# One PSUM bank moved from the ring of scores and projections to the ring that ScalarE empties

## The chip, the cores and the metric

The kernel runs on one core of one Trainium2 chip. The metric is the device time of one execution in microseconds (us), lower is better. The engines are TensorE (PE in the rows, with its weight loads as PEld), VectorE (DVE), ScalarE (ACT), GpSimd (POOL) and the DMA queues, which SyncE (SP) issues here.

## The reference, cut to what matters

Sixteen sequences of 256 rows with 128 channels go through a small wavelet and linear-attention stage (the prologue), and then through four layers of attention and mixture of experts:

```
for l in range(4):
    h = rms(x, ln1[l]); q, k, v = h @ wq[l], h @ wk[l], h @ wv[l]      # 16 query heads, 4 key heads of 64
    q, k = rope(q), rope(k)
    p = softmax(q k^T / 8 + causal_bias)                                # 256 x 256 for each head
    x = clip(x + (p v) @ wo[l], -100, 100)
    h = rms(x, ln2[l]); 2 of 8 experts for each row, by softmax(h @ wr[l])
    x = clip(x + sum(share_e * (silu(h wg_e) * (h wu_e)) @ wd_e), -100, 100)
out = x1 + gb * x
```

## The kernel before, in words

Every engine has its own program, written out by hand, and semaphores tie them together. The main part is a loop over 64 steps, one for each layer and sequence (`it`), and in each step TensorE's program mixes work of three steps: the scores of `it`, the last half of the attention of `it - 1`, and the projections of `it + 1`. The attention of a step falls into four blocks `q` of four heads.

TensorE's row of work in a step is: scores(it, 0), place 0, attend(it-1, 2), place 1, scores(it, 1), attend(it-1, 3), the projection of v, place 2, the output projection, place 3, turn_h, scores(it, 2), project_qk(it+1) outputs 0 to 5 (with the transposes of the routed rows after output 3), place 4, attend(it, 0), the router's logits, place 5, scores(it, 3), place 6, project_qk outputs 6 to 9, attend(it, 1), the ranks, place 7. The eight places hold pieces of the experts' work of the eight steps before: an even piece transposes rows and gated values, an odd one computes gate, up and down products. Of each eight steps (numbered 0 to 7 by `it % 8`, from `it` = 9 on), step 1 has pieces in places 4 to 7, steps 2 to 4 in all places, steps 5 and 6 in all but place 6, steps 7 and 0 in none. Pieces are odd in the odd places in steps 1 to 5, and the other way round in step 6 in places 0 to 5.

A block of attention goes like this:

- `scores` (L719 on, products at L734): for the heads i = 0, 2 of the block it computes the short product of head i (128 keys), that of head i + 1, then the long products (256 keys) of both, which tell VectorE that the bank is full. Each head has a PSUM bank.
- `mask_and_max` on VectorE (L1547, L1549): reads each head's bank twice, adds the mask and takes the maximum, and frees the bank; `L1553` then gives the negated maxima.
- `exps` on ScalarE (L1030), `invert` on VectorE (L1558), `normalise` on GpSimd (L1264).
- `attend` on TensorE: for each of the four heads three transposes into one bank (L759), which `copy_probs` on ScalarE copies out (L1037); then `weigh` for heads 0 and 1 when the copy of head 1 is done, and for heads 2 and 3 when the copy of head 3 is done (L777, L779).

`project_qk` (L807 to L809) gives each of its ten outputs a bank, which `rope` on VectorE (L1527) reads and frees; on VectorE rope of outputs 0 to 5 comes after the mask and maximum of block 2, and rope of outputs 6 to 9 after those of block 3, after invert(it, 2) and after what VectorE does of place 6.

The eight banks are three rings. The s ring holds scores, q/k projections and the output projection. The t ring holds the transposed probabilities, v, the transposed h and routed rows, logits, ranks and the experts' y, all of which ScalarE empties. The u ring holds the weighed values and the experts' rows, gate and gated values. `number_slots` counts the uses of each ring in TensorE's order; use n takes bank n modulo the ring's size, and TensorE waits until use n minus the ring's size has been read. The wait for a head's scores bank is:

```
def bank_is_free(i):
    at_least(pe, "s_free", S_AT["head", it, q, i] - S_RING + 1)
```

Of the kernel before, what the change touches and what calls it, by code (L numbers as in the profile page):

```python
# [207 lines left out]
def bass_program(nc, I, out):  # L208
    ctx = ExitStack()
    with ctx:  # L210
# [207 lines left out]

        half_steps = half_step_places()
        S_AT, T_AT, U_AT = number_slots(half_steps)  # L420
        S_RING, T_RING, U_RING = 4, 2, 2

        def s_bank(key):
            return S_AT[key] % S_RING
# [1348 lines left out]
```

How the kernel before makes its waits and increments, by code:

```python
        def phase_done(eng, k):  # L405
            eng.wait_ge(sem("phase_end"), PH * (k + 1))
# [1 line left out]
        def at_least(eng, name, n):  # L409
            if n > 0:
                eng.wait_ge(sem(name), n)
# [19 lines left out]
        def s_is_full(eng, key):  # L432
            eng.wait_ge(sem("s_full"), S_AT[key] + 1)
# [1 line left out]
        def t_is_full(eng, key):  # L435
            eng.wait_ge(sem("t_full"), T_AT[key] + 1)
# [1 line left out]
        def u_is_full(eng, key):  # L438
            eng.wait_ge(sem("u_full"), U_AT[key] + 1)
# [1 line left out]
        def s_was_read(eng, key):  # L441
            eng.wait_ge(sem("s_free"), S_AT[key] + 1)
# [1 line left out]
        def t_was_read(eng, key):  # L444
            eng.wait_ge(sem("t_free"), T_AT[key] + 1)
# [1 line left out]
        def u_was_read(eng, key):  # L447
            eng.wait_ge(sem("u_free"), U_AT[key] + 1)
# [28 lines left out]
        @block.sync  # L477
# [19 lines left out]
            def load_wv(l):  # L497
                load(wv, I["wv"][l], "wv_in")
            def load_wo(l):
                load(wo, I["wo_blocks"][l].rearrange("(c p) n -> p c n", p=P), "wo_in")
            load_wv(0)
            load_wo(0)
            load(wr, I["L0_ffn_wr"].rearrange("l h n -> h l n"), "wr_in")
            sp.wait_ge(sem("zeros_ready"), 1)
            for rows in rows_in + rows_out:
                for q in range(ZERO_PIECES):
                    sp.dma_start(zero_piece(rows, q), zeros).then_inc(sem("rows_zeroed"), 16)
            for h in range(2):
                sp.wait_ge(sem("x1_ready"), h + 1)
                sp.dma_start(x1_kept[:, half(h), :], x1[:, half(h), :]).then_inc(sem("x1_stored"), 16)
            def load_piece(it):
```

## Time and profile before

| | us |
|---|---|
| median of 3 runs | 3653.08 (3648.91 to 3657.68) |
| the profiled execution | 3653.33 |
| its span | 3651.5 |
| prologue, up to the scores of step 0 | 244.25 |
| steps 0 to 8 (no experts' pieces) | about 372 |
| last eight steps' experts and output, after the loop | 236.5 |
| TensorE busy | 2906.2 |
| mean granted TensorE clock | 0.906 |

The profile is of one execution. An instruction's row has its start from the span's beginning, its duration, its engine and line; in brackets stands the idle time of the engine just before it, and what ended it. Matmuls are pipelined, and their ends are modelled, so that two rows can overlap. The granted clock is 1.00 at 2.4 GHz and 0.50 at 1.2 GHz.

### The profile page before, as it was taken

The page shows a single profiled execution, that of the slowest core. Times are in us where ns is not written, and L with a number is a line of the kernel's source. Part 1 is how long each engine was busy: PE and PEld are TensorE (multiplying, and loading weights), DVE is VectorE, ACT ScalarE, POOL GpSimd, SP SyncE. Part 2 cuts the span into 40 slices and gives each one's busy share as a digit, 9 for nine tenths or more (in the row PEclk, how much of TensorE's full clock was granted, in tenths as well). Part 3 has the DMA queues.
Part 4 walks back from the last instruction along what each step waited for, and adds up shares of the span by engine and source line. Part 5 has one row for each costly group of instructions (what it writes and reads, how often), then busy time and mean ns, then how long its engine had stood idle before and what let it go on. Part 6 is the DMA issues. An engine that isn't in the chain of part 4 may idle for free.

```text
span 3651.5 us, 69801 instructions
## 1 busy us (share of the span) xinstructions
PE 2906.2 (80%) x22326; PEld 2366.8 (65%) x22326; DVE 2193.6 (60%) x8164; ACT 2016.6 (55%) x7089; POOL 1858.4 (51%) x1671
## 2 busy tenths in 40 slices
PE   5238887888888887888888987888888988888673
PEld 2226666777667766777667766777667766777462
DVE  5775555665556655665556665666566665666343
ACT  3026666566655665665656565656566665656321
POOL 0035655444655466554655556554655565555413
PEclk9569999999999999999999999999999999999775
DMA  9110101443145421543245421453145411442374
GB/s 375 74 41 31 35 33 59 146 150 122 52 133 175 153 84 61 169 148 117 67 136 169 155 78 61 164 165 97 67 137 179 163 56 62 153 154 80 115 251 137
DMA packets 270444, 438.36 MB, mean 120 GB/s; under 512 B 36305, under 2 KB 155633, under 8 KB 268657
## 3 DMA queue, kind: packets, MB, share of 16 engines
q1 hardware_dynamic: 253696, 400.31, 33.1%
q0 software_dynamic: 16384, 33.59, 3.0%
q8 instruction: 182, 2.98, 0.3%
q14 instruction: 182, 1.48, 0.1%
HBM read 323.13 MB, written 110.62 MB: 119 GB/s over the span
## 4 chain that ended last, share of the span: by engine, by line
PE 58%; ACT 19%; DVE 10%; POOL 6%; issue 3%; DMA 2%; SPq 1%; POOLq 0%; DVEq 0%
ACT arena L1030 10%; PE psum L759 7%; PE psum L777 7%; PE psum L807 5%; PE psum L808 4%; PE psum L809 4%; PE psum L734 4%; PE psum L779 3%; PE psum L827 3%; ACT arena L1037 3%; PE psum L877 3%; PE psum L878 2%; PE psum L879 2%; PE psum L903 2%; PE psum L902 2%
## 5 line engine op out<-in xcount | busy, mean ns | idle before, releaser
L1264 POOL TENSOR_TENSOR arena<-arena 128x512 f32<-128x512 f32 (+1 forms) x512 | 744.0, 1475 | 729.6 <-DVE arena L1558 727.7
L1030 ACT ACTIVATE arena<-arena 128x128 f32<-128x128 f32 (+1 forms) x2048 | 901.0, 446 | 23.6 <-DVE arena L1553 23.6
L759 PE MATMUL psum<-arena 128*128 128x128 f32 x3072 | 475.5, 292 | 259.0 <-ACT arena L1037 230.7
L759 PEld LDWEIGHTS psum<-arena 128*128 128x128 f32 x3072 | 342.9, 145 | 373.0 <-ACT arena L1037 293.4
L1037 ACT COPY arena<-psum 128x384 f32<-128x384 f32 x1024 | 445.5, 480 | 237.7 <-PE psum L759 236.7
L1562 DVE COPY arena<-psum 128x512 f32<-128x512 f32 x256 | 177.1, 692 | 618.4 <-PE psum L779 616.3
L734 PE MATMUL psum<-arena 64*128 64x128 f32 (+1 forms) x4096 | 453.5, 365 | 0.1
L1549 DVE CUSTOM_DVE_ANT_0 arena<-psum,arena 128x256 f32<-128x256 f32 x1024 | 430.2, 420 | 0.0
L807 PE MATMUL psum<-h_hi,wqk_hi 128*128 128x256 f32 x1280 | 392.8, 307 | 45.2 <-DVE arena L1549 43.7
L1527 DVE TENSOR_TENSOR arena<-psum,arena 128x512 f32<-128x512 f32 x640 | 406.0, 681 | 26.2 <-PE psum L809 21.3
L1280 POOL TENSOR_TENSOR arena<-arena 128x512 f32<-128x512 f32 x320 | 400.6, 1278 | 8.7 <-DVE arena L1527 8.6
L1030 ACT ACTIVATION_READ_ACCUMULATOR arena<-arena 128x1 f32 x2048 | 390.3, 191 | 0.0
L808 PE MATMUL psum<-h_hi,wqk_lo 128*128 128x256 f32 x1280 | 372.8, 291 | 0.0
L809 PE MATMUL psum<-h_lo,wqk_hi 128*128 128x256 f32 x1280 | 371.4, 290 | 0.0
L777 PE MATMUL psum<-arena 128*64 128x256 f32 x2048 | 368.2, 442 | 0.0
L734 PEld LDWEIGHTS psum<-arena 64*128 64x128 f32 x4096 | 321.3, 205 | 50.8 <-issue 25.6
L1255 POOL DMA_INDIRECT rows_in<-arena x256 | 256.2, 1001 | 150.3 <-DVE arena L1606 91.7
L807 PEld LDWEIGHTS psum<-h_hi,wqk_hi 128*128 128x128 f32 x1280 | 255.7, 200 | 93.1 <-issue 87.0
L1547 DVE CUSTOM_DVE_ANT_0 arena<-psum,arena 128x128 f32<-128x128 f32 x1024 | 294.0, 287 | 22.9 <-PE psum L734 15.7
L808 PEld LDWEIGHTS psum<-h_hi,wqk_lo 128*128 128x128 f32 x1280 | 256.6, 200 | 0.0
L809 PEld LDWEIGHTS psum<-h_lo,wqk_hi 128*128 128x128 f32 x1280 | 253.9, 198 | 0.0
L1112 ACT ACTIVATE arena<-psum 128x512 f32<-128x512 f32 x160 | 95.4, 596 | 270.5 <-PE psum L879 268.0
(199 smaller groups left out, 5711.0 us busy)
## 6 DMA issues: line engine op xcount, KB each, us to landing
gu<-gu_kept SPq DMA_DIRECT2D x320, 512.0 KB, 4.3
wd<-wd_kept SPq DMA_DIRECT2D x320, 256.0 KB, 3.9
arena<-rows_in SPq DMA_DIRECT2D x320, 64.0 KB
rows_out<-arena SPq DMA_DIRECT2D x320, 64.0 KB
rows_in<-arena SPq DMA_DIRECT2D x34, 512.0 KB, 7.8
rows_out<-arena SPq DMA_DIRECT2D x34, 512.0 KB, 7.1
gu_kept<-w_hi SPq DMA_DIRECT2D x32, 256.0 KB
gu_kept<-w_lo SPq DMA_DIRECT2D x32, 256.0 KB
```

The costliest lines, as they stand in the source:

```text
L734: return T.matmul(psum[:, s_bank(("head", it, q, i)), cols], QKT[par][r, 2 + 2 * q + i // 2, rows * P:(rows + 1) * P], QKT[par][r, q // 2, ...
L759: mm = T.transpose(psum[:, t_bank(key), j * P:(j + 1) * P], probs[:, q, i, j * P:(j + 1) * P], ident)
L777: return T.matmul(psum[r, bank, c0:c0 + S], v[:, 0, kv], pt[:, 0:S], start=True, stop=False, skip_group_check=True)
L807: T.matmul(out, wqk_hi[:, cols], h_hi, start=True, stop=False)
L808: T.matmul(out, wqk_lo[:, cols], h_hi, start=False, stop=False)
L809: mm = T.matmul(out, wqk_hi[:, cols], h_lo, start=False, stop=True)
L1030: ins = A.activation(a, a, ACT.Exp, bias=negmax[:, q, k:k + 1], accum_out=rowsum[:, q, k:k + 1])
L1037: A.copy(probsT[:, 4 * (q % 2) + i, :], psum[:, t_bank(key), 0:3 * P]).then_inc(sem("t_free"), 1)
L1264: ins = G.tensor_tensor(a, a, r[:, :, t:t + 1].broadcast_to([P, 4, P * (t + 1)]), ALU.mult)
L1280: G.tensor_tensor(QKT[it % 2][:, 2 * u:2 * u + 2, :].rearrange("p a b -> p (a b)"), own_part[:, k, :], turned_part[:, k, :], ALU.add).then ...
L1527: V.tensor_tensor(dst.rearrange("p (i s) -> p i s", i=2), psum[:, s_bank(("qk", it, m)), :].rearrange("p (i s) -> p i s", i=2), table.rear ...
L1549: V.tensor_tensor_reduce(probs[:, q, i, P:3 * P], psum[:, s_bank(key), P:3 * P], mask, SCALE, -3.0e38, ALU.add, ALU.max, rowmax[:, q, 2 * ...
```

## The change: ring sizes

```
-        S_RING, T_RING, U_RING = 4, 2, 2
+        S_RING, T_RING, U_RING = 3, 3, 2
```

That is the whole diff. Every engine's instructions stay the same and in the same order. What differs are bank numbers and the values that TensorE's waits for a free bank compare with: a use of the s ring now waits for the reading of the use three before it, not four, and a use of the t ring for the reading of the use three before it, not two. The u ring keeps banks 6 and 7. The prologue names its banks itself.

## Rows read from the trace of the kernel before

**Rows 1.** The page, busy time of an engine and share of the span.

```profile
PE 2906.2 (80%) x22326; PEld 2366.8 (65%) x22326; DVE 2193.6 (60%) x8164; ACT 2016.6 (55%) x7089; POOL 1858.4 (51%) x1671
```

**Rows 2.** The page, the chain that ended last, by engine.

```profile
PE 58%; ACT 19%; DVE 10%; POOL 6%; issue 3%; DMA 2%; SPq 1%; POOLq 0%; DVEq 0%
```

**Rows 3.** Waits of TensorE: us in total, times, longest.

```profile
PE psum L759 <- ACT arena L1037: 230.7, 240, 2.8
PE psum L792 <- ACT arena L1063: 221.0, 64, 68.1
PE psum L807 <- DVE arena L1549: 43.7, 60, 1.9
```

**Rows 4.** Stretches: steps 8 to 62, then step 50, step 51.

```profile
core 0: us, PE busy (x) PEld busy (x) DVE busy (x) ACT busy (x) POOL busy (x), PEclk, DMA share, GB/s
573.91:3371.60 2797.69, 2400.71 (x19040) 1968.12 (x19037) 1728.13 (x6857) 1694.71 (x6044) 1549.41 (x1387) 0.94 0.37 121
...
2696.83:2749.33 52.50, 46.05 (x383) 38.60 (x382) 34.92 (x130) 33.49 (x116) 29.24 (x27) 1.00 0.54 174
2749.33:2804.85 55.52, 49.07 (x382) 40.61 (x381) 34.86 (x130) 33.59 (x116) 29.31 (x27) 0.94 0.51 164
```

**Rows 5.** Timeline of TensorE, attend(36, 1): start, us, idle before.

```profile
2039.86 0.82 PE L759 MATMUL psum<-arena 128*128 128x128 f32 x6
2040.91 0.93 PE L759 MATMUL psum<-arena 128*128 128x128 f32 x6 [0.24 <-ACT arena L1037]
...
2042.48 0.60 PE L777 MATMUL psum<-arena 128*64 128x256 f32 x4
```

**Rows 6.** Timeline of ScalarE in the same block.

```profile
2040.38 0.86 ACT L1037 COPY arena<-psum 128x384 f32<-128x384 f32 x2 [0.71 <-PE psum L759]
2041.50 0.86 ACT L1037 COPY arena<-psum 128x384 f32<-128x384 f32 x2 [0.26 <-PE psum L759]
```

**Rows 7.** Timeline, scores(39, 0), and VectorE waiting for them.

```profile
2153.38 1.58 PE L734 MATMUL psum<-arena 64*128 64x128 f32 x16
...
2154.34 0.29 DVE L1547 CUSTOM_DVE_ANT_0 arena<-psum,arena 128x128 f32<-128x128 f32 x1 [0.54 <-PE psum L734]
```

**Rows 8.** Timeline, scores(36, 2) and what follows on both engines.

```profile
2020.57 1.58 PE L734 MATMUL psum<-arena 64*128 64x128 f32 x16
2022.67 0.36 PE L807 MATMUL psum<-h_hi,wqk_hi 128*128 128x256 f32 x1 [0.52 <-DVE arena L1549]
...
2021.89 0.28 DVE L1547 CUSTOM_DVE_ANT_0 arena<-psum,arena 128x128 f32<-128x128 f32 x1
...
2024.42 3.71 DVE L1527 TENSOR_TENSOR arena<-psum,arena 128x512 f32<-128x512 f32 x6
```

**Rows 9.** Timeline, scores(36, 3), last output projected (L807), mask, rope.

```profile
2034.74 1.58 PE L734 MATMUL psum<-arena 64*128 64x128 f32 x16
2039.13 0.28 PE L807 MATMUL psum<-h_hi,wqk_hi 128*128 128x256 f32 x1
...
2035.70 0.29 DVE L1547 CUSTOM_DVE_ANT_0 arena<-psum,arena 128x128 f32<-128x128 f32 x1
...
2040.21 2.47 DVE L1527 TENSOR_TENSOR arena<-psum,arena 128x512 f32<-128x512 f32 x4
```

**Rows 10.** Timeline of TensorE, the third head's transposes in attend(35, 3), attend(36, 2).

```profile
2008.80 0.92 PE L759 MATMUL psum<-arena 128*128 128x128 f32 x6 [2.02 <-ACT arena L1037]
...
2051.52 0.92 PE L759 MATMUL psum<-arena 128*128 128x128 f32 x6 [2.20 <-ACT arena L1037]
```

**Rows 11.** Timeline of TensorE, output 6 in step 38, without place 6.

```profile
2145.48 0.36 PE L807 MATMUL psum<-h_hi,wqk_hi 128*128 128x256 f32 x1 [0.97 <-DVE arena L1549]
```

**Rows 12.** Timeline, scores(38, 0) and their mask; GpSimd's normalise(40, 3) in step 41.

```profile
2100.78 1.58 PE L734 MATMUL psum<-arena 64*128 64x128 f32 x16
...
2102.75 0.28 DVE L1547 CUSTOM_DVE_ANT_0 arena<-psum,arena 128x128 f32<-128x128 f32 x1
...
2245.75 2.90 POOL L1264 TENSOR_TENSOR arena<-arena 128x512 f32<-128x512 f32 x2 [0.38 <-DVE arena L1558]
```

## The prediction

> **What bounds the kernel now.** I read the busy times first, then the chain that ended last, TensorE's waits, and the timeline of steps 36 to 41 piece by piece. TensorE is busy 80% of the span [rows 1] and holds 58% of the chain, ScalarE 19%, VectorE 10% [rows 2]: a step is a relay in which TensorE mostly works, and now and then waits for ScalarE. Two of its waits are long in total: third and later transposes of a block for ScalarE's copies (231 us, 240 times), and turn_h for scaled rows (221 us, one of 68 us in the prologue); that for a scores bank is 44 us [rows 3]. A step with pieces in all places takes 52.50 us at a granted clock of 1.00, and 55.52 us at 0.94 [rows 4], the same work.
>
> **The t ring, 2 to 3.** In a block the first two heads' transposes start at 2039.86, the third's only at 2040.91, after the first copy [rows 5]. ScalarE copies two heads in 0.86, then idles until 2041.50, and copies the other two by 2042.36 [rows 6]; the last weighing starts at 2042.48 [rows 5]. With a third bank the third head is transposed at once, the four copies run on end: two rows of 0.86 less an overlap, a copy every 0.38, so that the last starts 1.14 after the first and not 1.50 (2041.50 + 0.38 - 2040.38). Its transposes, started when the first copy ends (0.48 + 0.06 after its start), have it full 0.52 later (2039.86 to 2040.38 is that latency), at 1.06, just in time. The gain is 0.37 a block. The same holds where ScalarE comes late, since its pause is inside the block. There are 256 blocks: 94.7. In steps without pieces the next block waits for GpSimd's scatter and normalise, which take no notice: I take off 15 blocks for steps 0 and the first eight, and 2 us for the step whose turn_h then waits for gathered rows. Left: -87 us. Bounds: 0 (if the last transposes miss their time) and -130 (0.5 a block).
>
> **The s ring, 4 to 3, inside a block.** Head 3's short product now waits until VectorE has read head 0 of the same block. Head 0's reading starts 0.96 after the block where VectorE is free (2153.38 to 2154.34) [rows 7], and a bank is back at TensorE 0.78 after its reading started (2021.89 to 2022.67) [rows 8]. Of the block's 1536 columns 640 are then left, 0.63 of about 1.5 us. So the block ends 0.96 + 0.78 + 0.63 = 2.37 after its start, not 1.5: 0.85 later. VectorE's third head, which it takes 1.1 after the first, comes 0.5 later. What follows depends on the block.
>
> Blocks 0 and 1: TensorE then idles 2.20 or 2.02 for ScalarE's first copy [rows 10], so 0.85 is hidden, and ScalarE is behind with earlier exponentials, so the later maxima are too. The cover is gone where VectorE comes late. In step 6 of eight it starts head 0 at 2102.75, 1.97 after the scores [rows 12], and the piece behind is an odd one, that ScalarE waits for: head 3 waits until 2103.53, 1.8 lost, and about 0.3 is given back since there the block behind also waited for the bank of y: +1.5, seven times. In step 1 VectorE first lays out the experts' tiles, and GpSimd's normalise waits for its reciprocal [rows 12] and sends for the rows that the rest of the step waits for: that is 0.5 late, and hides its two attention gains (0.75): +1.2, seven times. Together +19.
>
> Block 2: the projection starts at 2022.67 already waiting for head 0 [rows 8]; now head 3 does, and the projection starts at 23.30, +0.63. Outputs 1 and 3 then wait for readings that are 0.5 late (rope starts at 2024.9 in place of 2024.42 [rows 8], and output 3 needs output 0 read): +0.2. Nothing waits longer behind it until attend(it, 0), for which ScalarE waits. +0.85, all 64 steps: +54. Bounds 0.5 and 1.1.
>
> Block 3: with place 6 filled and even (steps 2 to 4, 21 in all) head 3 starts at 2035.70 + 0.78 = 2036.48 and the scores end 0.85 late. The last output, at 2039.13 before, could start at 2039.98, but needs output 6 read, and rope starts at 2040.21, 0.62 each [rows 9]: 2040.21 + 0.62 + 0.15 = 2040.98. Rope waits for ScalarE's exponentials and piece, which this doesn't move. +1.85: +39. In step 1 the same with VectorE 1.2 later: +1.75, seven times, +12. In the other 36 steps output 6 already waits for head 0 [rows 11]; it starts 0.66 later, and output 9 waits for rope of output 6, itself 0.5 late: +0.9: +32. Block 3 together +84, all on the path, since attend(it, 1) has ScalarE waiting 0.71 [rows 6]. Bounds 50 and 110.
>
> Sum without the clock: -87 + 19 + 54 + 84 = +70.
>
> **The clock.** Steps 50 and 51 differ by 3.0 us through clocks of 1.00 and 0.94, and the 2797.69 us of the main part have 0.94 in the mean [rows 4]: by that ratio low stretches cost about 151 us there now. They follow TensorE's long idles, among them the 2.0 to 2.2 us before the third head's transposes [rows 10]. The change breaks those in two, 0.85 in the scores and about 1.0 before the fourth head: fewer low stretches behind blocks 0 and 1. It lengthens the idle around block 2 (a wait before turn_h stays, and 1.2 in the scores joins it) and makes new ones in block 3. I take -25 and +15. The estimate is rough, from no row of the new idles; bounds -90 and +60.
>
> Sum +60 on the profiled execution's 3653.33, which stands at the median of the runs (3653.08): 3713 us.
>
> **The rivals.**
> A, the other side: the clock. If the low stretches behind waits nearly all go, and block 2 and 3 make none, the clock gives more than 70 back, and the kernel is faster. It decides from 47 fewer stretches of 1.5 us each (half of 3.0). For it: the 2.0 to 2.2 idles do stand before many slow weighings. Against: turn_h's waits, 221 us in total [rows 3], stay, and what is slow behind them stays slow. If 100 of the 151 went: 3653 + 70 - 100 = 3623.
> B: more clock loss. The new pauses of 0.85 in each scores block, close to other waits, pull the clock down in blocks 2 and 3, where TensorE sets the pace: one stretch of 1.5 in half of 64 steps, +48, and none lost: 3653 + 70 + 48 = 3771. For it: step 36's slow weighings come after mere 2 us of idle.
> The Trainium skill, "TensorE: Matmul & The Clock Gate", section "A second HAM failure mode: psum-queue depth-cycling", says that short pauses of the PE between groups of matmuls, from cycling through PSUM banks, make its clock swing between the two levels and cost throughput. By that rule B is the likelier, and the sum would be about +118; the rows show swings now (0.94) behind idles of 2 us, and no row shows one behind a pause of 0.85 alone.
> C: the scores' waits are hidden. If VectorE's readings come so early that blocks 2 and 3 lose only the projection's 0.5 in block 2 (+32): 3653 - 87 + 32 = 3598. Against it: VectorE starts head 0 at the earliest 0.96 after the block begins, while head 3 is wanted at about 0.9.
> D: the rings are no limit and nothing moves: 3653. Against it: both waits stand in the rows.
>
> **How the numbers follow.** My forecast has 0.72 (its own range 3678 to 3745), B 0.13, A 0.08, C 0.03, D 0.04. A difference under 0.2%, 7 us, can't be told from none. Faster takes A and C less what of A ends near zero, 0.10; same 0.04; slower 0.86. The range leaves out C, most of A and the far part of B: 3668 to 3758.
>
> **What would show it.** In the profile after: inside a block the copies (L1037) run on end, four at 0.38, and TensorE's wait for them falls from 231 us to near 120; L734 shows idle on VectorE's L1549 in nearly all 256 blocks, about 0.8 each, some 200 to 250 us; L807 waits on L1527 or L1549 once in block 3, about 1 us in steps 2 to 4; step 50 takes about 53.8 at a clock of 1.00. Wrong would be: L734 not waiting, the fourth output of block 3 not waiting for rope, or a main-part clock above 0.97 (A) or under 0.92 (B).

## The result, and the profile after

The change makes the kernel slower: 3734.15 us (3733.45 to 3734.92, 4 runs) against 3655.3 (3648.91 to 3657.68, 4 runs beside it), a ratio of 1.0219 [1.0201, 1.0236]. The forecast was 3713 with a range of 3668 to 3758, so the result lies inside it, 21 us above the likeliest value. The profiled execution after takes 3733.57 us, 80.24 more than that of before, with a span of 3731.8 and a mean granted clock of 0.904 (0.906 before).

The busy times and the chain of the page of after, which answer to [rows 1, 2]:

```profile
PE 3011.5 (81%) x22326; PEld 2469.1 (66%) x22326; DVE 2201.8 (59%) x8164; ACT 1991.7 (53%) x7089; POOL 1860.7 (50%) x1671
...
PE 56%; ACT 18%; DVE 12%; POOL 7%; issue 4%; DMA 2%; SPq 1%; POOLq 0%; DVEq 0%
```

The counts are the same. TensorE's busy time is 105 us longer for the same work, because the modelled rows are longer: a block's scores, one row of 1.58 before [rows 9], are two rows of 1.14 and 0.92 with a pause between them, and at the low clock the first of the two takes 1.76 (both shown below). In the chain VectorE has gone from 10 to 12%.

TensorE's waits after (us in total, times, longest), which answer to [rows 3]:

```profile
PE psum L792 <- ACT arena L1063: 213.4, 64, 68.1
PE psum L734 <- DVE arena L1549: 207.4, 257, 4.4
PE psum L759 <- ACT arena L1037: 54.1, 70, 1.9
...
PE psum L807 <- DVE arena L1527: 14.3, 21, 0.7
```

The wait for ScalarE's copies has fallen from 231 us to 54. In its place stands one that did not exist: the scores (L734) wait for VectorE's reading of the same block, 257 times, 207 us. The projection no longer waits for the scores' banks (44 us before), only 21 times for rope, which are the steps 2 to 4 with place 6 filled.

Step 50 after, to be set beside its 52.50 in [rows 4]:

```profile
2767.14:2820.88 53.74, 47.93 (x383) 39.83 (x382) 34.97 (x130) 33.07 (x116) 29.54 (x27) 1.00 0.53 170
```

Now a block as it runs. TensorE, scores(35, 1) with attend(34, 3) behind it, after (start, us, idle before):

```profile
2001.14 1.14 PE L734 MATMUL psum<-arena 64*128 64x128 f32 x10
2002.80 0.92 PE L734 MATMUL psum<-arena 64*128 64x128 f32 x6 [0.52 <-DVE arena L1549]
2003.65 1.20 PE L759 MATMUL psum<-arena 128*128 128x128 f32 x9
2005.55 0.55 PE L759 MATMUL psum<-arena 128*128 128x128 f32 x3 [0.70 <-ACT arena L1037]
```

The idle of 2.0 us before the third head's transposes [rows 10] is in pieces: 0.52 inside the scores, 0.70 before the fourth head. Three heads are now transposed on end (x9). Block 3 of the same step, the last two outputs of the projection and attend(35, 1):

```profile
2033.22 0.92 PE L734 MATMUL psum<-arena 64*128 64x128 f32 x6 [0.52 <-DVE arena L1549]
...
2037.76 0.39 PE L807 MATMUL psum<-h_hi,wqk_hi 128*128 128x256 f32 x1 [0.68 <-DVE arena L1527]
...
2038.58 1.61 PE L759 MATMUL psum<-arena 128*128 128x128 f32 x12
```

and ScalarE's copies of that block, which answer to [rows 6]:

```profile
2039.10 1.63 ACT L1037 COPY arena<-psum 128x384 f32<-128x384 f32 x4 [2.61 <-PE psum L759]
```

Four copies take 1.63 on end; before it was 0.86, a pause of 0.26, and 0.86. That is the gain. The projection's wait for rope, 0.68, and the scores' 0.52 are the price in this block.

**Where the time went, step by step.** I cut a step at four points: first product of scores(it, 0), first product of scores(it, 1), turn_h (L792), first product of scores(it, 3). The four pieces hold blocks 0, 1, 2 and 3 in this order. First two steps before, 44 at full clock and 51 with low stretches (columns as in [rows 4]):

```profile
2399.99:2410.59 10.60, 8.39 (x70) 6.48 (x69) 5.91 (x24) 6.92 (x24) 8.89 (x9) 1.00 0.87 281
2410.59:2426.38 15.79, 12.73 (x105) 10.85 (x104) 8.88 (x32) 12.61 (x49) 5.19 (x6) 1.00 0.42 134
2426.38:2440.95 14.57, 13.64 (x112) 11.78 (x112) 10.27 (x40) 6.42 (x18) 8.77 (x8) 1.00 0.37 122
2440.95:2452.46 11.51, 11.27 (x98) 9.47 (x97) 9.61 (x36) 7.32 (x26) 5.94 (x5) 1.00 0.49 160
2749.33:2761.34 12.01, 9.80 (x69) 7.61 (x68) 5.81 (x24) 6.92 (x24) 9.99 (x10) 0.86 0.86 277
2761.34:2778.74 17.40, 14.33 (x106) 11.74 (x105) 8.89 (x32) 12.71 (x49) 4.06 (x5) 0.90 0.39 125
2778.74:2793.33 14.59, 13.66 (x112) 11.80 (x112) 10.54 (x40) 6.63 (x18) 9.33 (x8) 1.00 0.38 122
```

Then two steps after, 35 at full clock, and 51:

```profile
1990.90:2001.14 10.24, 8.84 (x69) 6.78 (x69) 6.17 (x24) 6.81 (x24) 8.25 (x9) 1.00 0.92 286
2001.14:2016.56 15.42, 13.16 (x105) 11.14 (x104) 8.98 (x32) 12.50 (x49) 5.43 (x6) 1.00 0.51 165
2016.56:2031.57 15.01, 14.06 (x113) 12.09 (x113) 10.69 (x40) 6.54 (x18) 9.34 (x8) 1.00 0.34 118
2031.57:2044.63 13.06, 11.86 (x99) 9.81 (x98) 9.30 (x36) 7.22 (x26) 6.30 (x5) 1.00 0.43 142
2820.88:2831.12 10.24, 8.84 (x70) 6.79 (x69) 5.90 (x24) 6.82 (x24) 8.28 (x9) 1.00 0.83 258
2831.12:2846.55 15.43, 13.17 (x105) 11.15 (x105) 8.98 (x32) 12.51 (x49) 5.44 (x6) 1.00 0.59 184
2846.55:2863.88 17.33, 16.94 (x113) 14.44 (x113) 10.84 (x40) 6.53 (x18) 9.35 (x8) 0.80 0.32 103
```

Read the clock column. In step 51 before, the low clock stands in pieces one and two (0.86, 0.90) and not in three. After, one and two run at 1.00, and piece three at 0.80, which costs 17.33 - 15.01 = 2.3 us. Compare the full-clock pieces of 44 and 35 to have the change alone: -0.36, -0.37, +0.44, +1.55, together +1.26.

Summed over the 63 steps whose four pieces are complete, after less before is -23.9, -50.2, +107.3 and +53.4 us, together +86.6; prologue and tail give -6.4. The time that the pieces spend at the low clock (worked out as in the next section) sums to 106, 103, 152 and 7 us before, and to 41, 12, 339 and 14 after. So block 2 had low stretches before the change too, and now has more than twice as much; blocks 0 and 1 lost three quarters of theirs. The sum over the loop has hardly moved (369 and 406 us), and the main part's mean clock is 0.94 in both.

### The profile page after: what moved, and what is told of

Read it like the earlier page. It is cut to its first block, busy times and chain, and to the rows that moved or that the text cites. A ratio compares the mean times of both kernels' runs of the same rounds, so it can differ in the third digit from the quotient of the medians.

```text
span 3731.8 us, 69800 instructions
## 1 busy us (share of the span) xinstructions
PE 3011.5 (81%) x22326; PEld 2469.1 (66%) x22326; DVE 2201.8 (59%) x8164; ACT 1991.7 (53%) x7089; POOL 1860.7 (50%) x1671
## 4 chain that ended last, share of the span: by engine, by line
PE 56%; ACT 18%; DVE 12%; POOL 7%; issue 4%; DMA 2%; SPq 1%; POOLq 0%; DVEq 0%
ACT arena L1030 10%; PE psum L759 7%; PE psum L777 6%; PE psum L734 5%; PE psum L807 5%; PE psum L808 4%; PE psum L809 4%; PE psum L827 3%; PE psum L779 3%; PE psum L877 3%; POOL rows_in L1255 2%; PE psum L879 2%; PE psum L878 2%; PE psum L903 2%; PE psum L902 2%
## 5 line engine op out<-in xcount | busy, mean ns | idle before, releaser
L734 PE MATMUL psum<-arena 64*128 64x128 f32 (+1 forms) x4096 | 588.5, 379 | 207.4 <-DVE arena L1549 207.4
L734 PEld LDWEIGHTS psum<-arena 64*128 64x128 f32 x4096 | 397.8, 202 | 307.2 <-DVE arena L1549 259.2
L1037 ACT COPY arena<-psum 128x384 f32<-128x384 f32 x1024 | 416.5, 489 | 272.6 <-PE psum L759 272.5
L759 PE MATMUL psum<-arena 128*128 128x128 f32 x3072 | 436.0, 284 | 74.2 <-ACT arena L1037 54.1
L759 PEld LDWEIGHTS psum<-arena 128*128 128x128 f32 x3072 | 342.7, 144 | 155.1 <-ACT arena L1037 100.6
L807 PE MATMUL psum<-h_hi,wqk_hi 128*128 128x256 f32 x1280 | 429.4, 335 | 15.8 <-DVE arena L1527 14.3
L808 PE MATMUL psum<-h_hi,wqk_lo 128*128 128x256 f32 x1280 | 401.8, 314 | 0.0
L807 PEld LDWEIGHTS psum<-h_hi,wqk_hi 128*128 128x128 f32 x1280 | 287.5, 225 | 71.6 <-issue 51.1
L777 PE MATMUL psum<-arena 128*64 128x256 f32 x2048 | 329.1, 400 | 0.0
L808 PEld LDWEIGHTS psum<-h_hi,wqk_lo 128*128 128x128 f32 x1280 | 288.5, 225 | 0.0
L809 PEld LDWEIGHTS psum<-h_lo,wqk_hi 128*128 128x128 f32 x1280 | 285.1, 223 | 0.0
L827 PE MATMUL psum<-arena 128*128 128x128 f32 x2048 | 240.0, 275 | 0.8 <-issue 0.8
```

Of the source, the lines that this page charges most:

```text
L734: return T.matmul(psum[:, s_bank(("head", it, q, i)), cols], QKT[par][r, 2 + 2 * q + i // 2, rows * P:(rows + 1) * P], QKT[par][r, q // 2, ...
L759: mm = T.transpose(psum[:, t_bank(key), j * P:(j + 1) * P], probs[:, q, i, j * P:(j + 1) * P], ident)
L777: return T.matmul(psum[r, bank, c0:c0 + S], v[:, 0, kv], pt[:, 0:S], start=True, stop=False, skip_group_check=True)
L807: T.matmul(out, wqk_hi[:, cols], h_hi, start=True, stop=False)
L808: T.matmul(out, wqk_lo[:, cols], h_hi, start=False, stop=False)
L809: mm = T.matmul(out, wqk_hi[:, cols], h_lo, start=False, stop=True)
```

## The experiments

The levels of the clock are 1.00 and 0.50, so that the time at the low level is 2 x (1 - mean clock) x span. The last column is of the profiled execution and is rough: executions of one kernel differ in mean clock by up to 0.014 with hardly a difference in time (before: 3655.45 us at 0.916, 3657.95 at 0.902, which is 100 us at the low level). Ratios are to the kernel before, run on the same chip. The four kernels e4c, e5c, e7c and e8c ran on a chip on which the kernel before takes 3763.94 us (3757.09 to 3774.22) and not 3655; only their ratios are compared. Even ratios don't carry over exactly: one and the same kernel, e7c and e9, has 1.0014 there and 0.9936 on another chip.

| kernel | us | ratio [95%] | clock | low level, us |
|---|---|---|---|---|
| before | 3655.3 | 1 | 0.906 | 686 |
| after (3, 3, 2) | 3734.15 | 1.0219 [1.0201, 1.0236] | 0.904 | 716 |
| e1, rings 3, 2, 2 | 3814.38 | 1.0437 [1.0419, 1.0456] | 0.905 | 725 |
| e2, after + head order | 3699.92 | 1.0135 [1.0109, 1.0160] | 0.915 | 629 |
| e3, third head in the s ring | 3548.45 | 0.9709 [0.9691, 0.9728] | 0.931 | 489 |
| e6, after + products before turn_h | 3689.5 | 1.0094 [1.0077, 1.0112] | 0.924 | 561 |
| e4c, scores' waits alone | 3935.33 | 1.0459 [1.0429, 1.0488] | 0.898 | 801 |
| e5c, projection's waits alone | 3844.62 | 1.0217 [1.0182, 1.0252] | 0.901 | 760 |
| e7c, before + products before turn_h | 3769.02 | 1.0014 [1.0000, 1.0028] | 0.911 | 670 |
| e8c, e3 + the same products | 3661.55 | 0.9712 [0.9675, 0.9750] | 0.926 | 541 |
| e9, the kernel of e7c on another chip | 3629.24 | 0.9936 [0.9914, 0.9958] | 0.927 | 531 |
| e10, e3 + head order | 3547.34 | 0.9709 [0.9696, 0.9723] | 0.924 | 539 |

**The two rings apart: e1_s3t2.** The smaller s ring alone; one bank lies idle.

```
-        S_RING, T_RING, U_RING = 4, 2, 2
+        S_RING, T_RING, U_RING = 3, 2, 2
```

> Rings of 3, 2 and 2: the s ring loses its bank, the t ring gets none, one bank lies idle. Theory (the third t bank is worth 87 us of work, and some 50 us more of clock, since it shortens the idle before the third head's transposes behind blocks 0 and 1): 3734 + 87 + 50 = about 3870 us, and the 2 us idles before L759 are back in place of 54 us in total. Rival (the third t bank hardly matters, the loss is nearly all of the s ring): under 3770.

Measured 3814.38 (3811.42 to 3817.14). The third t bank is thus worth 3814.38 - 3734.15 = 80 us, and the lost s bank costs 160. By pieces, the t bank's part is 23.7, 15.5, 15.4, 24.7. In steps at full clock it is 0.33 to 0.38 in each of the four (step 50: 10.61, 15.80, 15.34, 13.43 in e1, and 10.25, 15.43, 15.02, 13.05 after). Piece two sums to less because in steps 7 and 0 of eight, which have no experts' pieces or nearly none, it takes 4.4 us longer after than in e1, as much as piece one gains there. I had expected about 3870, with 50 us of clock on top of the 87 for the bank: that clock didn't show, the low-level time is 725 us beside 716. Waits of TensorE in e1:

```profile
PE psum L734 <- DVE arena L1549: 204.3, 257, 4.4
PE psum L759 <- ACT arena L1037: 122.7, 234, 2.5
```

The scores wait as in after, so that wait is the s ring's; the wait for copies has lost only what the late scores now hide.

**The s ring's two customers apart: e4c_wait_scores, e5c_wait_qk.** Rings 4, 2, 2, with one kind of wait as strict as with three banks.

```
e4c  -  at_least(pe, "s_free", S_AT["head", it, q, i] - S_RING + 1)
     +  at_least(pe, "s_free", S_AT["head", it, q, i] - 3 + 1)
e5c  -  at_least(pe, "s_free", S_AT[key] - S_RING + 1)        # project_qk
     +  at_least(pe, "s_free", S_AT[key] - 3 + 1)
```

> The kernel before with its rings of 4, 2 and 2, and only the waits of the scores made as strict as with three s banks (the use three before must be read). This is the part of the s ring inside a block, alone. Theory (a pause in every block, hidden in blocks 0 and 1, not in 2 and 3): about 0.8 each in blocks 2 and 3, 1.2 to 1.8 in block 0 of steps 1 and 6, that is some 118 us, and with clock 3790 to 3820 us; L734 waits about 205 us for L1549. Rival (most of the loss is the projections' waits for banks): under 3720.

> The kernel before with rings of 4, 2 and 2, and only the waits of project_qk as strict as with three s banks. Theory (block 2: output 0 waits for head 1 in place of head 0, 0.4 to 0.5; block 3: output 9 waits for rope of output 6, 1.85 in steps 2 to 4, about 1.6 in step 1, 0.5 elsewhere): about 97 us, 3740 to 3760 us; alone it costs less than the scores' part, and both alone add to more than the 160 us by which three s banks without a third t bank are slower, since in block 3 one wait covers the other. Rival (it costs a few tens of us, and the scores' part is all): under 3700.

The strict scores' waits alone give about the whole loss of e1 (1.0459 beside 1.0437, on different chips; expected 1.037 to 1.045); the projection's alone give 1.0217 (expected 1.023 to 1.029). The sum of both, 6.8%, is more than e1's 4.4%, by more than the 0.8% that the chip made for e7c and e9: they overlap. The third and fourth piece, which differ by 0 and 5 us in sum between the two chips (e7c and e9), say the same: over the kernel before, e1 has +123 and +78 us there, e4c +115 and +60, e5c +29 and +73. Where the scores have waited for their bank, the outputs of the projection mostly need not. In e5c the projection waits 112 us, in after only 14:

```profile
PE psum L807 <- DVE arena L1549: 75.0, 75, 2.1
...
PE psum L807 <- DVE arena L1527: 37.2, 35, 1.5
```

Both ratios hold what that chip does to the kernel as well, and I don't convert them into microseconds of the first.

**Head order: e2_order.** Rings 3, 3, 2; both products of a head before the next head's, so that VectorE's third head isn't late.

```
-                for i in (0, 2):
-                    bank_is_free(i)
-                    product(i, 0, P)
-                    bank_is_free(i + 1)
-                    product(i + 1, 0, P)
-                    product(i, 1, 2 * P).then_inc(sem("s_full"), 1)
-                    product(i + 1, 1, 2 * P).then_inc(sem("s_full"), 1)
+                for i in range(4):
+                    bank_is_free(i)
+                    product(i, 0, P)
+                    product(i, 1, 2 * P).then_inc(sem("s_full"), 1)
```

> The changed kernel, with the four heads' products in head order: both products of head 2 are issued before the wait for head 3's bank. Theory (the wait sits in the middle of the second pair, so that head 2's scores come 0.5 us late to VectorE and 0.63 us of work are left behind the wait): VectorE's heads come on time, 0.38 us are left, about 0.25 to 0.5 less in blocks 2 and 3 except where rope of output 6 decides (steps 2 to 4): 3734 - 40 = about 3695 us, and VectorE's waits for L734 (L1547, 99 us) go below 40. Rival (only head 3's bank counts, not the order): 3725 to 3740.

The time is as expected, 3699.92 (3696.55 to 3711.47), and so is VectorE's wait for the scores (32 us in place of 99, expected under 40), but the time doesn't come from there. TensorE's wait falls:

```profile
PE psum L734 <- DVE arena L1546: 88.6, 108, 4.0
```

Yet a full-clock step is as long as in after (piece three 14.98 in step 35 and 15.01). Of the 38 us gained in the loop 31 lie in piece three, where the low-level time falls from 339 to 262 us: the gain is the clock's. So the late third head of VectorE, to which I gave part of the loss, costs nothing measurable.

**The pause before block 2: e6_fill.** Rings 3, 3, 2; four products of constants into the bank of h, just before turn_h waits for ScalarE.

```
-                pe.wait_ge(sem("z_ready"), it + 1)
                 t_is_free(("h", it))
+                for k in range(4):
+                    T.matmul(psum[:, t_bank(("h", it)), 0:S], ident, cosT, start=True, stop=True)
+                pe.wait_ge(sem("z_ready"), it + 1)
```

> The changed kernel, with four products of constants (identity by the cosine table, 256 columns each, about 0.9 us together) issued into the bank of the transposed h before the wait for its rows, and overwritten there: extra work that leaves the output as it is. Theory (block 2's part costs 107 us and not the 31 counted because TensorE's idle before turn_h and the new one inside the scores together bring the clock down in block 2): the clock there stays at 1.00 in steps 2 to 6, and the time falls by 30 to 60 us, to about 3690. Rival (block 2's extra is waits for readings, not clock): 3734 to 3750, the granted clock of step 51 stays at 0.94 or below.

Measured 3689.5 (3685.45 to 3693.14): 45 us faster than after for more work. Step 51 in e6, in the same four pieces:

```profile
2785.97:2796.21 10.24, 8.85 (x70) 6.80 (x69) 5.90 (x24) 6.81 (x24) 8.28 (x9) 1.00 0.80 246
2796.21:2812.19 15.98, 14.77 (x113) 12.65 (x113) 8.98 (x32) 13.03 (x52) 5.43 (x6) 1.00 0.60 190
2812.19:2827.15 14.96, 14.01 (x113) 12.04 (x111) 10.69 (x40) 5.93 (x14) 9.34 (x8) 1.00 0.34 115
2827.15:2840.20 13.05, 11.86 (x98) 9.81 (x97) 9.31 (x36) 7.22 (x26) 6.29 (x5) 1.00 0.44 143
```

The products make turn_h late (15.98, not 15.43), and piece three is back at 1.00 (14.96, not 17.33). What stands before and behind turn_h in after and in e6, TensorE's rows in step 51, after first:

```profile
2846.55 0.44 PE L792 MATMUL psum<-arena 128*128 128x128 f32 x2 [1.05 <-ACT arena L1063]
2846.92 1.76 PE L734 MATMUL psum<-arena 64*128 64x128 f32 x10
2848.99 1.65 PE L734 MATMUL psum<-arena 64*128 64x128 f32 x6 [0.31 <-DVE arena L1549]
```

```profile
2810.42 1.94 PE L791 MATMUL psum<-arena 128*128 128x256 f32 x8
2812.19 0.38 PE L794 MATMUL psum<-arena 128*128 128x128 f32 x2
2812.50 1.14 PE L734 MATMUL psum<-arena 64*128 64x128 f32 x10
2814.52 0.92 PE L734 MATMUL psum<-arena 64*128 64x128 f32 x6 [0.87 <-DVE arena L1551]
```

The pause inside the scores is there in e6 too, 0.87, and in total (216 us beside 207); by itself it doesn't bring the clock down. Nor does the pair of idles each time. In step 51 after, the clock is down already in the first ten products behind turn_h (1.76, and 1.14 at full clock), before the pause in the scores has begun. And step 35 after has both idles, 1.05 and 0.87, in a piece at 1.00:

```profile
2016.56 0.44 PE L792 MATMUL psum<-arena 128*128 128x128 f32 x2 [1.05 <-ACT arena L1063]
2016.93 1.14 PE L734 MATMUL psum<-arena 64*128 64x128 f32 x10
2018.94 0.92 PE L734 MATMUL psum<-arena 64*128 64x128 f32 x6 [0.87 <-DVE arena L1549]
```

What is shown is the sum. At the low level piece three spends 152 us before and 147 in e3, which have the idle before turn_h and no pause in the scores; 262 in e2, whose scores pause 89 us in all; 339 after and 322 in e1, whose scores pause 207 and 204; and 163 in e6. In steps 2 to 5 of eight from step 10 on, whose idle before turn_h four products fill, it is 38 before, 99 after and 0 in e6. So in these steps the idle before turn_h has to be there, and the scores' pauses add to what it does. How the two act together in one step isn't shown.

**The same products with rings 4, 2, 2: e7c_fill_before, e9_fill_before.** Their number is sized to the step, from 2 to 13.

```
+                u = (it - 1) % HB if it > HB + 1 else 7
+                for k in range({1: 13, 2: 2, 3: 2, 4: 2, 5: 2, 6: 5, 7: 7, 0: 7}[u]):
+                    T.matmul(psum[:, t_bank(("h", it)), 0:S], ident, cosT, start=True, stop=True)
```

> The kernel before, with products of constants in the idle before turn_h, written to the bank of the transposed h and overwritten there: 2 in steps 2 to 5, 5 in step 6, 7 in steps 7 and 0 and the first, 13 in step 1 (0.4 us each by the run with four). Extra work that leaves the output as it is. It prices the clock that block 2 already lost before the change. Theory (some of the 151 us of clock loss of the kernel before stand there): 3655 - 35 = about 3620 us. Rival (the idle before turn_h does no harm where nothing is added to it): 3650 to 3660.

> The same kernel as e7c_fill_before: rings 4, 2, 2 and constant products just before turn_h. Theory (the clock alone is what the filling products gave in e6_fill, whatever the rings): the low-clock stretches behind turn_h get shorter also with rings 4, 2, 2, low-clock time falls from 689 us to under 600, and the kernel takes about 3620 us (ratio 0.985 to 0.995); the ratio of 1.0014 in e7c_fill_before was then that chip. Rival: without a pause inside the scores of block 2 the idle before turn_h makes few low stretches by itself, so the products give nothing back: ratio 0.998 to 1.004, low-clock time above 650 us.

The first gave nothing, 1.0014, and I took the theory to be refuted for these rings. I had expected 35 us. The second, the same kernel on another chip, gave 0.9936, 24 us, a little more than the noise, as the theory says (expected 0.985 to 0.995, and under 600 us at the low level). In the profiled executions its gain is in piece three (-46 us against before) and piece one (-6), and much of it is lost again in pieces two (+18) and four (+19). The products empty piece three of low stretches on both chips: 4.9 us at the low level in e9 and 5.5 in e7c, where the kernel before has 152, and the piece takes 828.5 us in both. Put together: with four s banks the filling gives back less (24 us) than with three (45), in line with the low-level time of piece three, 152 us beside 339; but the number of products differs as well, and what they cost elsewhere isn't taken apart.

**The third head in the s ring: e3_third_in_s, e8c_third_fill, e10_third_order.** If the t ring wants a third bank only for the third head of a block, that head can borrow one of four s banks, with a count of its own for ScalarE's reading.

```
+                    if i == 2:
+                        s_is_free(pe, key)
+                        bank, name = s_bank(key), "s_full"
+                    else:
+                        t_is_free(key)
+                        bank, name = t_bank(key), "t_full"
```

> Rings of 4, 2 and 2 as before, but the third head's transposes of each attention block take a use of the s ring, with a count of its own for what ScalarE has read there. Theory (the gain of the third t bank and the loss of the s bank are separable, and the s ring has a free bank when attention is transposed): the copies run on end as in the changed kernel, gain 0.37 in the blocks but attend(it, 1) of steps 2 to 4, where the use waits for rope of output 6: 75 us, and about 50 of clock: 3655 - 125 = about 3530 us, no idle in L734 on L1549. Rival (ScalarE and the places take the gain back): 3620 to 3655.

> The version with the third head's transposes in the s ring (3548 us), with the same products of constants before turn_h, sized to the idle. Extra work that leaves the output as it is. Theory (block 2 is where this version still loses clock, 0.931 in the mean): 3548 - 40 = about 3508 us, the granted clock over steps 8 to 62 near 0.99. Rival (the products make turn_h late, as 0.56 each step in the run with four): 3540 to 3560.

> Rings 4, 2, 2, the third head's transposes in a bank of the s ring, and the scores' products head by head. Theory: head by head order has VectorE's reading of the third head 0.3 us earlier where a bank is short, and with four banks only the third head's slot makes one short, so little is left to gain: 3535 to 3550 us, within 0.5% of e3_third_in_s (3548). Rival: head order takes away a stretch of products that covered the wait for head 3's bank, or gives VectorE its first head later in no case and its second earlier, and moves the clock as in e2_order: 3510 to 3530 us.

e3 is the best kernel of this case: 3548.45 (3543.14 to 3551.19), 107 us under the kernel before and 186 under the changed one (expected about 3530). Its pieces of step 35 take 10.23, 15.43, 14.19 and 11.53 us, with the clock at 1.00: blocks 0 to 2 have the t ring's gain, the scores run without a pause, and only block 3 has none, since there the borrowed bank is still being read by rope (L1556). TensorE in that block, attend(35, 1) (L782 and L830 are the lines L759 and L807 of before):

```profile
1939.44 0.82 PE L782 MATMUL psum<-arena 128*128 128x128 f32 x6
1940.56 0.88 PE L782 MATMUL psum<-arena 128*128 128x128 f32 x6 [0.30 <-DVE arena L1556]
```

By pieces e3 has -38, -25, -22 and -17 us against before. Low-level time falls by 197 us as well, but 65 of them lie in the prologue, which takes the same 244 us with them or without; 137 lie in the loop. How the 107 us divide between 0.37 a block and the clock no run here tells. Head order adds nothing to e3 (0.9709). The filling products with it have 0.9712, where I had expected 40 us more than e3 gives, but e8c ran only on the chip on which they gave the kernel before nothing either, and its piece three is 48 us shorter than that of e3 (804.8 and 852.5): what they would give on the chip of e3 is open.

## Why the prediction was right, and where it was off

**The t ring (-87).** Right: 80 by e1, 0.36 and 0.37 in the full-clock pieces, copies on end at 0.38. The 7 us between come on top of the 7.7 that I had taken off (15 blocks and 2 us): the gain in piece one of steps 7 and 0 is lost again in piece two (4.4 us), and I had taken off such blocks only up to step 8.

**The s ring inside a block.** Head 3 waits for VectorE as worked out. In scores(35, 3) the pause is the 0.52 shown before the row at 2033.22, and the row ends at 2034.14, 2.57 after the block's start at 2031.57: 1.0 later than the 1.58 of [rows 9], not 0.85. VectorE's third head is 0.3 late, not 0.5, and e2 shows that this doesn't matter. In step 6, which I gave +1.5 in block 0, the full-clock pieces of before and e1 show +1.28 (9.58 and 10.86). The +1.2 for step 1 stands in no piece at full clock on both sides.

**Block 2 (+54) and block 3 (+84).** Right, from full-clock pieces of steps 35 and 44, where the t ring's 0.37 is taken out: block 2 has 0.44 + 0.37 = 0.81 (said 0.85), block 3 in steps 2 to 4 has 1.55 + 0.37 = 1.92 (said 1.85), through the output that waits for rope, 21 times, 0.68 each (said about 1). In the other steps block 3 has 0.7 to 1.0 (said 0.9), in step 1 1.57 (said 1.75). Step 50 at full clock: 53.74, forecast about 53.8. The terms without clock, +70, hold: e1 has the s ring at +160 with its clock, the sum of my terms 19 + 54 + 84 = 157. Its loop has 41 us more at the low level than before, by the price of step 51 an estimated 14 us, so about 146 stand beside the 157.

**The clock (-25 + 15 = -10).** The step that failed, in size and in place. With +70 taken off, the profiled +80.24 leave +10. By pieces, what isn't accounted for by my terms (about -21 for blocks 0 and 1, +30 for block 2, +60 for block 3, with the t ring's gain shared out at 24 a block and what I took off it counted in blocks 0 and 1) is -54, +77 and -7, with -6 outside the loop. The low-level time has the same signs: -156, +187 and +7 us. So the relief behind blocks 0 and 1 was twice what I took, and the new loss in block 2 five times. That the forecast came within 21 us is in this part luck: two errors, 29 us one way and some 60 the other, took each other back in part. I had written that the change lengthens the idle around block 2; I priced it with block 3's at 15 us. e6 shows that the idle before turn_h is needed for the loss: with it filled, 45 us come back though the scores still pause (-68 in piece three, +26 in the two beside it). e2 and e3 show that the scores' pauses are needed too: fewer of them, and piece three has less low-level time.

**TensorE's wait for the copies.** Forecast near 120, measured 54. The late scores take the rest off: e1, with two t banks, has 122.7, where before had 230.7. It had no price of its own in the sum.

**The rivals.** A (the clock gives more than 70 back) is the truth of blocks 0 and 1 alone, -54, and block 2 took it back. B (+118 through more low stretches) has the right place, block 2, and less than the size there, 77 us where it had 48; what failed is its "and none lost", since the stretches behind blocks 0 and 1 went. In the loop the low-level time grew by 38 us, which at the price seen in step 51 (2.3 us for 17.33 x 0.20 x 2 = 6.9 at the low level) is an estimated 13 us of loss and not 48. That agrees with the +10 left above. The page's rule that I set beside it, of the Trainium skill, "TensorE: Matmul & The Clock Gate", section "A second HAM failure mode: psum-queue depth-cycling", holds here only in part: pauses of 0.5 in the scores of blocks 1 and 3 stand in pieces with a clock of 1.00, and one of 0.87 does in e6; in block 2, where another idle stands right before, the low-level time grew with them. C fell: the scores' waits are in the profile 257 times. D fell by the ratio.

What stays open: how much of e3's gain is clock, and why the low stretches take turns between steps (35 has none after, 51 has one, with the same instructions and the same 1.05 before turn_h).

## What to carry to other kernels

Banks moved between two rings are two changes, and can be priced apart: what the one ring gains is a pause of the reader inside each block (0.37, here 80 us), what the other loses is the time from the product to the bank's return (160 us). A ring that holds one block's heads exactly must not be cut by one: the last head then waits for the first reader of its own block. That is hidden only where a longer wait follows in any case, as here in blocks 0 and 1 of most steps. Before a bank is moved, ask whether the one use that wants it can borrow a slot in the other ring: that gave 3% where the move cost 2%.

Where a change breaks up or joins idles of TensorE, sum the low-level time by the place of each idle and not over the kernel: here a sum of +38 us was -156 in two places and +187 in a third. Ask of each new pause what idle stands next to it.

## What the runs showed of the hardware

One kernel's time and clock differ between chips. e7c and e9 are the same program, 3769 and 3629 us. Step 36, from scores(36, 0) to scores(36, 1), in e9 and then in e7c:

```profile
1981.70:1993.72 12.02, 9.81 (x69) 7.54 (x68) 5.90 (x24) 6.92 (x24) 10.00 (x10) 0.86 0.90 285
...
2051.87:2066.27 14.40, 11.05 (x69) 8.44 (x68) 6.10 (x24) 7.27 (x24) 10.28 (x10) 0.76 0.79 246
```

The steps' instructions are the same, and so are TensorE's rows up to the second head's transposes. Then TensorE waits longer in e7c. The third head's transposes, e9 and e7c:

```profile
1986.94 0.92 PE L759 MATMUL psum<-arena 128*128 128x128 f32 x6 [2.21 <-ACT arena L1040]
...
2058.27 1.54 PE L759 MATMUL psum<-arena 128*128 128x128 f32 x6 [3.35 <-ACT arena L1040]
```

ScalarE's copy comes 1.1 later, mostly because ScalarE stood still twice before it, where in e9 it has no pause. The profile knows no engine of this core that ended the two idles:

```profile
2056.45 0.47 ACT L1110 ACTIVATE xT_hi<-psum,arena 128x256 fp32r<-128x256 f32 x1 [0.59 <-remote]
2057.25 0.59 ACT L1119 CAST hh_hi<-psum 128x512 fp32r<-128x512 f32 x1 [0.32 <-remote]
```

Such idles of ScalarE and VectorE, 76 us in all in e7c, are in each of the four traces of this chip and in none of the others. So the low clock there (0.76 in place of 0.86) comes behind a longer idle of TensorE, 3.35 and not 2.21. Of the 127 us by which e7c's loop is longer, 88 lie in this piece and 34 in the next, none in the third; at the low level the loop spends 348 us beside 215. How the 3% divide between these idles and the clock, and where the idles come from, no run here tells. An experiment of half a per cent, as e7c, can come out differently on such a chip.
